# Delta rule of a four-layer kernel: sums for the norms of q and k on four column groups in two batches, and two steps of the query convolution one turn later

## The chip, the cores and the metric

The kernel runs on one core of a Trainium2 chip. The metric is the time of one execution on the device in microseconds, as the median of several runs. One core has TensorE (matrix products into PSUM), VectorE, ScalarE and GpSimd, and queues for transfers. The profile calls them PE (and PEld for its weight loads), DVE, ACT and POOL.

## The reference

Four layers run one after another on x with 8 samples of 512 tokens and 128 channels. The change touches one half of the last layer alone, a gated delta rule. Cut to what matters:

```python
q = _causal_dw_conv_silu(x @ Wq, conv_q).reshape(bsz, seq_len, H, KD)   # H = 8 heads, KD = 128
k = _causal_dw_conv_silu(x @ Wk, conv_k).reshape(bsz, seq_len, H, KD)
v = _causal_dw_conv_silu(x @ Wv, conv_v).reshape(bsz, seq_len, H, VD)   # VD = 32
q = _l2norm(q)        # x / max(sqrt(sum(x * x)), 1e-6), over the 128 numbers of a head
k = _l2norm(k)
def step(state, inp):
    q_t, k_t, v_t, a_t, b_t = inp
    retained = jnp.einsum('bhvk,bhk->bhv', state, k_t)
    state = a4 * (state - b4 * retained[..., None] * k_t[:, :, None, :]) + b4 * v_t[..., None] * k_t[:, :, None, :]
    o_t = jnp.einsum('bhvk,bhk->bhv', state, q_t)
```

All arithmetic is in float32. The convolution has four taps. The sums of squares of q and of k over a head's 128 numbers are what the change computes in another way.

## The kernel before

`delta_rule` splits the layer into 16 **units**: a sample of 512 tokens and four of its eight heads (`u // 2` is the sample, `u % 2` the half of the heads). A unit has 4 **chunks** of 128 tokens. The recurrence over 128 tokens becomes a triangular system per chunk. Its 32 x 32 blocks are inverted by small products (L2045, with VectorE's X and Y and ScalarE's F between them), and then the chunk is solved: L2088 multiplies by an inverted block, VectorE copies the result to `d_W` (L2371), L2081 takes it to the next block, VectorE subtracts it from `d_r` (L2368), four times over; then VectorE makes zz (L2374) and ze (L2377), and TensorE uses them in L2094 and L2098.

The order is written out as **turns**. `in_turn` walks through them, and every engine's program is that walk with only its own instructions. The list `INVERT` has NI = 9 steps, so 9 turns invert one chunk, and 36 turns a unit. While chunk n is inverted, chunk n - 1 is solved (`SOLVE`, also 9 steps), and chunk n + 1 is made (`make`, in turns 0, 3 and 6 of the nine): TensorE's L2030 and L2038, VectorE's `d_D` and `d_A` (L2316, L2321, L2326, L2329), ScalarE's `d_D` and its four copies of `d_A` (L2228), GpSimd's `d_D` (L2187) and its two products `d_M` (L2192), which the next chunk's inversion needs. I call nine such turns a **room**, and number the rooms of a unit 0 to 3, the turns in it 0 to 8. Room 0 solves the last chunk of the unit before, which has no ze and no L2098.

Around that, `pieces_at` puts the preparation of later units into turns, each with a place: 0 ahead of the solve step, 1 behind it, 2 at the end of the turn. For a unit there are eight **runs** (x = 0 to 7): q and k of each of four heads. For an even run (q) TensorE makes one product over 512 columns (L2132), ScalarE scales it into `d_conv` (L2259, step j = 0), VectorE adds the other three taps, one instruction each (L2409, steps j = 1 to 3, over 511, 510 and 509 columns), and ScalarE applies Silu. For an odd run (k) TensorE makes four products (L2136) and ScalarE applies Silu at once. GpSimd squares the result (L2214) into one of four buffers `d_sq`. Then TensorE adds the squares over the 128 partitions, one product each (L2144): its moving operand is the squares (512 columns), its stationary operand 8 columns of `picks` that pick the output row, so that eight products, accumulated in the bank `few`, leave eight rows. VectorE copies these rows out (L2442), and four products (L2148) turn them so that tokens lie on partitions.

Preparation runs some one and a half units ahead. For a unit inverted in rooms 0 to 3, each room holds one even and one odd run of a later unit: its sums stand in turn 3 (even x) and turn 5 (odd x), its convolution steps j = 0 to 3 in turns 4, 4, 5 and 7. The gates, the value products (L2121, L2122 in turn 4), the keys' transposes (L2162 in turn 7 of rooms 0, 2 and 3), the norm of the output and, for every second unit, the output projection (L2170 and L2175, in room 1) stand between.

Every engine works its list off strictly in order, and waits are semaphore counts. In GpSimd's list the squaring of run x waits until the sum that last read its buffer is done.

## Time and profile before

| what | us |
|---|---|
| median of 3 runs (lowest, highest) | 4025.28 (4021.14, 4027.91) |
| the profiled run | 4018.16 |
| its span on the core | 4016.4 |
| busy in the span: PE, DVE, ACT, POOL | 3464.0, 2409.0, 1597.0, 538.5 |
| stage of the delta units | from 2476 to about 3937 |

The profiled run has a time of its own, 1.8 us over its span, and stands 7.1 us under the median. A row of a timeline gives the start from the span's start, the duration, engine and line, output and inputs with their shapes, and how many records it merges; in brackets the idle time of the engine before it and what ended it. A product in float32 leaves two records, one for each of two passes (x8 is four products); a transpose leaves one.

### The profile page before, as it was taken

To read this page: it belongs to the slowest core of one execution; us is meant where nothing else is said; L and a number is where in the kernel's file an instruction comes from. 1 tells how busy PE (TensorE), PEld (TensorE's weight loads), DVE (VectorE), ACT (ScalarE), POOL (GpSimd) and SP (SyncE) were. 2 spreads that over 40 slices of the span, in tenths; PEclk is the share of its full clock that TensorE was granted. 3 is DMA by queue.
4 is the path that set the end of the run, shared out by engine and by line. 5 is a ranking of instruction groups with operands and counts; after the bars stand their busy time and mean duration, and the time that the engine had idled before them with its cause. 6 is when DMAs were issued, how large, how long until landed. Compare 5 with 4: busy or idle time off the path is not lost. (4 is left out here: it accounts for less than half of the span.)

```text
span 4016.4 us, 124072 instructions
## 1 busy us (share of the span) xinstructions
PE 3464.0 (86%) x55256; PEld 2180.0 (54%) x55256; DVE 2409.0 (60%) x6248; ACT 1597.0 (40%) x2941; POOL 538.5 (13%) x564
## 2 busy tenths in 40 slices
PE   3877777678999999999978796999999999999985
PEld 1336665224545555555556342666666666666772
DVE  3757777328777667767785112565666666666545
ACT  1663333345444444444320343444444344434323
POOL 0212222000000000000000000222222222222210
PEclk9986667789989888888765897999999999999967
DMA  2000000111111111111000001000000000000000
GB/s 89 0 0 1 1 1 1 44 65 59 45 34 45 42 45 37 41 44 35 14 3 3 16 0 44 2 3 3 2 3 2 3 2 3 3 3 3 2 2 23
DMA packets 37029, 77.11 MB, mean 19 GB/s; under 512 B 7696, under 2 KB 11152, under 8 KB 35472
## 3 DMA queue, kind: packets, MB, share of 16 engines
q1 hardware_dynamic: 36496, 69.17, 5.3%
q8 instruction: 437, 7.16, 0.7%
q14 instruction: 96, 0.79, 0.1%
HBM read 64.83 MB, written 4.33 MB: 17 GB/s over the span
## 5 line engine op out<-in xcount | busy, mean ns | idle before, releaser
L1369 PE MATMUL ps<-g_hs,g_fc 128*128 128x512 f32 x448 | 275.2, 699 | 55.1 <-DVE g_hs L1683 39.6
L1260 PEld LDWEIGHTS ps<-g_Q,g_K 32*32 32x32 f32 x12288 | 205.4, 120 | 184.1 <-issue 97.8
L1491 ACT ACTIVATE g_hidden<-ps 128x512 f32<-128x512 f32 x224 | 133.2, 595 | 419.4 <-PE ps L1369 417.7
L2136 PE MATMUL ps<-d_hp,d_w_k 128*128 128x512 f32 x512 | 280.3, 634 | 0.0
L1260 PE MATMUL ps<-g_Q,g_K 32*32 32x32 f32 (+1 forms) x12288 | 236.6, 227 | 27.4 <-DVE g_H L1529 10.1
L1383 PE MATMUL ps<-g_hidden,g_proj 128*128 128x512 f32 x448 | 256.6, 660 | 0.0
L2214 POOL TENSOR_TENSOR d_sq<-d_QK 128x512 f32<-128x512 f32 x128 | 133.7, 1044 | 912.8 <-ACT d_QK L2265 751.6
L2234 ACT ACTIVATE d_F<-ps 128x128 f32<-128x128 f32 x256 | 70.9, 277 | 347.4 <-PE ps L2045 344.2
L1228 POOL COPY g_xb<-X 128x512 f32<-128x512 f32 x8 | 7.3, 908 | 1217.4 <-DVE X L1689 1105.9
L2409 DVE SCALAR_TENSOR_TENSOR d_conv<-ps,w_conv_q,d_conv 128x511 f32<-128x511 f32 (+2 forms) x192 | 142.4, 742 | 36.8 <-ACT d_conv L2259 33.0
L2192 POOL TENSOR_TENSOR d_M<-d_A,w_joins 128x128 f32<-128x128 f32 (+1 forms) x128 | 114.3, 912 | 342.8 <-ACT d_A L2228 342.8
L2045 PE MATMUL ps<-d_X,d_M 32*32 32x32 f32 x8192 | 123.7, 196 | 39.7 <-DVE d_X L2341 20.0
L794 PE MATMUL ps<-att_kg,att_qx 32*128 32x96 f32 x1024 | 121.7, 354 | 42.0 <-DVE att_qx L708 27.4
L2038 PE MATMUL ps<-d_QK 128*128 128x128 f32 x1024 | 153.6, 295 | 0.0
L2368 DVE TENSOR_TENSOR d_r<-d_r,ps 32x128 f32<-32x128 f32 x192 | 55.0, 286 | 161.4 <-PE ps L2081 89.6
L2045 PEld LDWEIGHTS ps<-d_X,d_M 32*32 32x32 f32 x8192 | 96.2, 108 | 100.0 <-issue 66.0
L1276 PEld LDWEIGHTS ps<-g_V,g_KT 32*32 32x32 f32 x4096 | 81.1, 121 | 126.1 <-issue 91.6
L1517 DVE TENSOR_TENSOR g_S<-g_S,ps 128x128 f32<-128x128 f32 x64 | 18.4, 288 | 215.5 <-PE ps L1276 215.2
L1493 ACT ACTIVATE g_hidden<-g_hidden 128x512 f32<-128x512 f32 x224 | 141.1, 630 | 7.2
L794 PEld LDWEIGHTS ps<-att_kg,att_qx 32*128 32x128 f32 x1024 | 115.5, 254 | 51.0 <-DVE att_qx L708 29.7
L1369 PEld LDWEIGHTS ps<-g_hs,g_fc 128*128 128x128 f32 x448 | 78.3, 206 | 119.4 <-DVE g_hs L1683 42.8
L771 ACT ACTIVATE att_pt<-ps 96x512 f32<-96x512 f32 x128 | 75.0, 594 | 169.6 <-PE ps L811 168.7
(479 smaller groups left out, 7938.8 us busy)
## 6 DMA issues: line engine op xcount, KB each, us to landing
g_hs<-gate_rows SPq DMA_DIRECT2D x56, 256.0 KB, 3.4
g_fc<-in_c_fc_dram SPq DMA_DIRECT2D x56, 256.0 KB, 4.1
g_proj<-in_c_proj_dram SPq DMA_DIRECT2D x56, 256.0 KB, 2.6
X<-in_x_dram SPq DMA_DIRECT2D x1, 2048.0 KB, 10.8
w_c_fc<-in_c_fc_dram SPq DMA_DIRECT2D x1, 2048.0 KB, 7.9
w_c_proj<-in_c_proj_dram SPq DMA_DIRECT2D x1, 2048.0 KB, 12.3
ex_root<-gate_rows SPq DMA_DIRECT2D x1, 2048.0 KB, 15.7
h_rows<-k SPq DMA_DIRECT2D x1, 2048.0 KB, 6.2
```

Of the source, the lines that this page charges most:

```text
L794: ins = e.matmul(scored[:, g, b], qx[ts(g, 32), q, 4 * u + b, :, :].rearrange("p h q -> p (h q)"), kg[ts(g, 32), q, 4 * u + b, :], start=T ...
L1260: ins = e.matmul(later(scored, n_), keys_, queries(n_, planes, r_, 4 * i + j), start=(turn_ == 0 and part == 0 and n_ != 1), stop=(part == 1),
L1369: e.matmul(P[2], fc[:, n % 2, ts(f, C)], hs[:, n % 2], start=True, stop=True).then_inc(pe.steps, pe.did(now(f"u{i}")))
L1383: e.matmul(P[3], proj[:, n % 2, f, :], r[:, (16 * c["half"] + i) % 5], start=(c["half"] == 0 and i == 0), stop=(c["half"] == 1 and i == 15 ...
L1491: e.activation(r[:, slot], P[2], ACT.Relu).then_inc(act.steps, act.did(now(f"r{i}")))
L1493: e.activation(r[:, slot], r[:, slot], ACT.Square).then_inc(act.steps, act.did(now(f"q{i}")))
L2038: ins = e.matmul(mk[:, ts(h, C)], QK[:, 1, H, t], QK[:, part - 1, H, t], start=True, stop=True)
L2045: ins = e.matmul(inv[rows, h], stationary[rows, h], moving[rows, h], start=True, stop=True, tile_position=(32 * j, 32 * j))
L2136: ins = e.matmul(b, w_k[:, j, ts(H, C)], hp_of(u)[:, j:j + T], start=(j == 0), stop=(j == TAPS - 1))
L2192: e.tensor_tensor(M[:, a, levels], A32[:, a].unsqueeze(1).to_broadcast([C, many, 4, 32]), k.w["joins"][:, levels].unsqueeze(2).to_broadcas ...
L2214: e.tensor_tensor(squares(x), qk, qk, ALU.mult).then_inc(pool.steps, pool.did(f"{tag}sq{x}"))
L2409: e.scalar_tensor_tensor(cv[:, late:], tap_bank(run)[:, 0:T - late], k.w["conv_q"][:, 4 * g + run // 2, 3 - late:4 - late], cv[:, late:], ...
```

## The change

- **Sums.** `squares` is now put twice a unit instead of eight times: for x = 3 and x = 7, in the turn where the sum of that run stood (turn 5 of rooms 0 and 2). Each time TensorE issues four products, one for each buffer of `d_sq`, each with a stationary operand of 32 columns and on a column group of its own (`tile_position=(0, 32 * j)`), so that product j writes the 32 partitions from 32 j on. The first batch starts the accumulation, the second ends it. `picks` becomes two matrices of 32 columns, of which the first column or the second one is ones. The sum of run x comes to stand in row 32 * (x % 4) + x // 4.
- **Rows.** `d_square_rows` has 128 rows instead of 8, and VectorE copies all of `few`. The four products that turn them take a new table `heads` (128 x 8) as their moving operand instead of the 8 x 8 corner of the identity, and contract 128 rows.
- **Waits.** GpSimd's squares wait for the batch that read the four buffers.
- **Convolution.** VectorE's steps j = 1 and 2 are put one turn later: turns 5 and 6 instead of 4 and 5. Step 3 stays in turn 7.

```diff
-                        put(u, NI * (x // 2) - 50 + (0, 0, 1, 3)[j], "conv", TAPS * x + j, place=(1 if j == 0 else 2))
+                        put(u, NI * (x // 2) - 50 + (0, 1, 2, 3)[j], "conv", TAPS * x + j, place=(1 if j == 0 else 2))
...
-                    put(u, NI * (x // 2) - 42 + 2 * (x % 2), "squares", x)
+                    if x % 4 == 3:
+                        put(u, NI * (x // 2) - 42 + 2 * (x % 2), "squares", x // 4)
...
-                            e.wait_ge(pool.steps, pool.at(f"{tag}sq{x}"))
+                            e.wait_ge(pool.steps, pool.at(f"{tag}sq{4 * x + 3}"))
                             if x == 0 and u:
                                 e.wait_ge(dve.steps, dve.at(f"u{u - 1}ssq"))
-                            row = 4 * (x % 2) + x // 2
-                            e.matmul(few[0:8, :], k.w["picks"][:, row, :], squares(x), start=(x == 0), stop=(x == 7)).then_inc(pe.steps, pe.did(f"{tag}ss{x}"))
+                            for j in range(4):
+                                ins = e.matmul(few[ts(j, 32), :], k.w["picks"][:, x, :], squares(j), start=(x == 0), stop=(x == 1), tile_position=(0, 32 * j))
+                            ins.then_inc(pe.steps, pe.did(f"{tag}ss{x}"))
...
-                                ins = e.matmul(few[:, ts(i, 8)], sq_rows[:, ts(i, C)], k.w["ident"][0:8, 0:8], start=True, stop=True)
+                                ins = e.matmul(few[:, ts(i, 8)], sq_rows[:, ts(i, C)], k.w["heads"][:], start=True, stop=True)
...
-                                e.wait_ge(pe.steps, pe.at(f"{tag}ss{x - 4}"))
+                                e.wait_ge(pe.steps, pe.at(f"{tag}ss0"))
                             elif u:
-                                e.wait_ge(pe.steps, pe.at(f"u{u - 1}ss{x + 4}"))
+                                e.wait_ge(pe.steps, pe.at(f"u{u - 1}ss1"))
...
-                            e.wait_ge(pe.steps, pe.at(tag + "ss7"))
-                            e.tensor_copy(sq_rows[:], few[0:8, :]).then_inc(dve.steps, dve.did(tag + "rows"))
+                            e.wait_ge(pe.steps, pe.at(tag + "ss1"))
+                            e.tensor_copy(sq_rows[:], few).then_inc(dve.steps, dve.did(tag + "rows"))
```

Lines of the changed file are one to five higher than those of the kernel before. TensorE's list in room 0, turns 3 to 5, before the change; L2144 is a sum, L2132 the query's product, L2081 and L2088 belong to the solving, L2045 to the inversion, L2121 and L2122 are the value products:

```order
L2132 MATMUL ps<-d_hp,d_w_q 128x512
L2144 MATMUL ps<-d_sq,w_picks 8x512
L2081 MATMUL ps<-d_W,d_A 32x32 x4
L2045 MATMUL ps<-d_F,d_Y 32x32 x16
L2121 MATMUL ps<-d_w_v,d_hp 128x128 x4
L2122 MATMUL ps<-w_Wg,d_hp 128x128
L2088 MATMUL ps<-d_r,d_Y 32x32 x4
L2045 MATMUL ps<-d_X,d_M 32x32 x16
L2144 MATMUL ps<-d_sq,w_picks 8x512
L2081 MATMUL ps<-d_W,d_A 32x32 x4
L2038 MATMUL ps<-d_QK 128x128 x4
```

The same turns of TensorE after the change:

```order
L2133 MATMUL ps<-d_hp,d_w_q 128x512
L2082 MATMUL ps<-d_W,d_A 32x32 x4
L2046 MATMUL ps<-d_F,d_Y 32x32 x16
L2122 MATMUL ps<-d_w_v,d_hp 128x128 x4
L2123 MATMUL ps<-w_Wg,d_hp 128x128
L2089 MATMUL ps<-d_r,d_Y 32x32 x4
L2046 MATMUL ps<-d_X,d_M 32x32 x16
L2145 MATMUL ps<-d_sq,w_picks 32x512 x4
L2082 MATMUL ps<-d_W,d_A 32x32 x4
L2039 MATMUL ps<-d_QK 128x128 x4
```

The sum of turn 3 is gone, and that of turn 5 is a batch of four. In room 2 the same holds, with the sum of turn 3 ahead of the query's product instead of behind it. In rooms 1 and 3 both sums are gone.

VectorE's list in room 3, turns 4 to 7, before the change; L2409 is the convolution:

```order
L2409 SCALAR_TENSOR_TENSOR d_conv<-ps,w_conv_q,d_conv 128x511
L2371 COPY d_W<-ps 32x128
L2409 SCALAR_TENSOR_TENSOR d_conv<-ps,w_conv_q,d_conv 128x510
L2368 TENSOR_TENSOR d_r<-d_r,ps 32x128
L2326 TENSOR_TENSOR d_D<-d_D,d_gam 128x512
L2329 TENSOR_TENSOR d_A<-ps,d_D 128x512
L2341 TENSOR_TENSOR d_X<-d_X,ps 128x128
L2343 STREAM_TRANSPOSE d_Y<-d_X 128x128
L2416 TENSOR_TENSOR d_values_gates<-d_values_gates,d_kn 128x128
L2371 COPY d_W<-ps 32x128
L2374 TENSOR_TENSOR d_zz<-d_W,d_gam 128x128
L2377 TENSOR_TENSOR d_ze<-d_zz,d_end 128x128
```

The same turns of VectorE after the change:

```order
L2373 COPY d_W<-ps 32x128
L2411 SCALAR_TENSOR_TENSOR d_conv<-ps,w_conv_q,d_conv 128x511
L2370 TENSOR_TENSOR d_r<-d_r,ps 32x128
L2328 TENSOR_TENSOR d_D<-d_D,d_gam 128x512
L2331 TENSOR_TENSOR d_A<-ps,d_D 128x512
L2343 TENSOR_TENSOR d_X<-d_X,ps 128x128
L2345 STREAM_TRANSPOSE d_Y<-d_X 128x128
L2418 TENSOR_TENSOR d_values_gates<-d_values_gates,d_kn 128x128
L2411 SCALAR_TENSOR_TENSOR d_conv<-ps,w_conv_q,d_conv 128x510
L2373 COPY d_W<-ps 32x128
L2376 TENSOR_TENSOR d_zz<-d_W,d_gam 128x128
L2379 TENSOR_TENSOR d_ze<-d_zz,d_end 128x128
```

The first convolution step has moved from ahead of the `d_W` copy to behind it, and the second from ahead of `d_r` to between the scaling of the values and the next `d_W` copy. It is the same in the other rooms.

## Rows read from the trace of the kernel before

**Rows 1.** Windows: stretch, engines busy (records), PE clock, DMA share, GB/s
```profile
2529.00:3767.00 1238.00, 1187.97 (x22567) 843.04 (x22567) 765.04 (x2277) 509.00 (x1131) 324.65 (x314) 1.00 0.01 3
```

**Rows 2.** Timeline of a room 3, turns 5 to 8, all engines
```profile
3383.26 0.34 PE L2088 MATMUL ps<-d_r,d_Y 32*32 32x32 f32 x5
...
3384.37 0.29 DVE L2371 COPY d_W<-ps 32x128 f32<-32x128 f32 x1
...
3385.47 0.29 DVE L2368 TENSOR_TENSOR d_r<-d_r,ps 32x128 f32<-32x128 f32 x1
...
3386.59 0.69 DVE L2329 TENSOR_TENSOR d_A<-ps,d_D 128x512 f32<-128x512 f32 x1
...
3387.74 0.25 DVE L2416 TENSOR_TENSOR d_values_gates<-d_values_gates,d_kn 128x128 f32<-128x128 f32 x1
...
3388.68 0.29 DVE L2377 TENSOR_TENSOR d_ze<-d_zz,d_end 128x128 f32<-128x128 f32 x1
3388.69 1.82 POOL L2192 TENSOR_TENSOR d_M<-d_A,w_joins 128x128 f32<-128x128 f32 x2 [5.05 <-ACT d_A L2228]
...
3389.27 0.97 PE L2094 MATMUL ps<-d_zz,d_P 128*128 128x32 f32 x8
```

**Rows 3.** Timeline of a room 0, turns 3 and 4, TensorE
```profile
3317.41 0.60 PE L2144 MATMUL ps<-d_sq,w_picks 128*8 128x512 f32 x1
3317.41 0.44 PE L2081 MATMUL ps<-d_W,d_A 128*32 128x32 f32 x8
...
3318.36 0.45 PE L2045 MATMUL ps<-d_F,d_Y 32*32 32x32 f32 x32
```

**Rows 4.** Timeline of the attention stage: 16 products on four column groups
```profile
424.66 1.08 PE L819 MATMUL ps<-att_pt,att_vt 96*32 96x128 f32 x32 [0.68 <-ACT att_pt L771]
```

**Rows 5.** Timeline of a room 2, turns 3 to 6, all engines
```profile
3008.86 1.02 PE L2144 MATMUL ps<-d_sq,w_picks 128*8 128x512 f32 x2
...
3009.81 1.12 PE L2132 MATMUL ps<-d_hp,d_w_q 128*128 128x512 f32 x2
...
3010.87 0.44 PE L2081 MATMUL ps<-d_W,d_A 128*32 128x32 f32 x8
...
3011.24 0.45 PE L2045 MATMUL ps<-d_F,d_Y 32*32 32x32 f32 x32
...
3011.34 0.28 DVE L2368 TENSOR_TENSOR d_r<-d_r,ps 32x128 f32<-32x128 f32 x1 [2.07 <-PE ps L2081]
...
3012.93 0.34 PE L2088 MATMUL ps<-d_r,d_Y 32*32 32x32 f32 x5
...
3013.40 0.29 DVE L2371 COPY d_W<-ps 32x128 f32<-32x128 f32 x1 [0.37 <-PE ps L2088]
3013.55 0.60 PE L2144 MATMUL ps<-d_sq,w_picks 128*8 128x512 f32 x1
...
3014.70 0.29 DVE L2368 TENSOR_TENSOR d_r<-d_r,ps 32x128 f32<-32x128 f32 x1 [0.23 <-PE ps L2144]
```

**Rows 6.** Timelines of two rooms 1; the first row's room has output
```profile
3258.81 0.97 PE L2094 MATMUL ps<-d_zz,d_P 128*128 128x32 f32 x8
...
3339.45 0.75 DVE L2409 SCALAR_TENSOR_TENSOR d_conv<-ps,w_conv_q,d_conv 128x511 f32<-128x511 f32 x1 [0.62 <-ACT d_conv L2259]
...
3342.45 0.69 DVE L2329 TENSOR_TENSOR d_A<-ps,d_D 128x512 f32<-128x512 f32 x1
...
3344.89 1.08 PE L2094 MATMUL ps<-d_zz,d_P 128*128 128x32 f32 x8
```

**Rows 7.** Timelines where VectorE meets GpSimd: a room 0, the last unit
```profile
3326.70 1.05 POOL L2214 TENSOR_TENSOR d_sq<-d_QK 128x512 f32<-128x512 f32 x1
3326.96 0.93 DVE L2391 TENSOR_TENSOR d_O<-d_o,d_qn 128x128 f32<-128x128 f32 x1
...
3888.78 1.72 POOL L2192 TENSOR_TENSOR d_M<-d_A,w_joins 128x128 f32<-128x128 f32 x2 [10.49 <-ACT d_A L2228]
...
3888.79 0.59 DVE L2377 TENSOR_TENSOR d_ze<-d_zz,d_end 128x128 f32<-128x128 f32 x1
```

More of the change, by code:

```diff
@@ L123 @@
     "gla": ["W_in2", "b_in2", "W_qka", "b_qka", "W_v2", "b_v2", "W_y2", "b_y2", "W_out2", "b_out2", "h0", "gla_mask"],
-    "delta": ["conv_q", "Wv3", "Wg3", "Wab3", "Wo3", "A_log", "dt_bias", "conv_v", "o_norm_w", "joins", "eye32", "upto3", "ones3", "picks"],
+    "delta": ["conv_q", "Wv3", "Wg3", "Wab3", "Wo3", "A_log", "dt_bias", "conv_v", "o_norm_w", "joins", "eye32", "upto3", "ones3", "picks", "heads"],
     "mix": ["W_r3", "W_k3", "W_v3", "mu"],
@@ L1855, in delta_rule @@
         ssq = k.sb("d_ssq", [C, 2, NT, NH], stack=s)
-        sq_rows = k.sb("d_square_rows", [8, T], stack=s)
+        sq_rows = k.sb("d_square_rows", [C, T], stack=s)
         cv = k.sb("d_conv", [C, T], stack=s)[:]
@@ L2744, in layouts @@
     o["upto3"], o["ones3"] = o["upto"].copy(), o["ones"].copy()
-    o["picks"] = rows(np.eye(8, dtype=np.float32))
+    o["picks"] = rows(np.eye(2, 32, dtype=np.float32))
+    o["heads"] = np.zeros((C, 8), np.float32)
+    for x in range(8):
+        o["heads"][32 * (x % 4) + x // 4, 4 * (x % 2) + x // 2] = 1.0
     for n in "rkv":
```

## The prediction

> **What bounds the kernel now.** I read first the windows view of the delta stage's steady part, then the timelines of TensorE, VectorE and GpSimd in the four kinds of nine-turn room that follow one another there, and last the rows in which VectorE and GpSimd meet. TensorE is busy for 1188 of 1238 us at a granted clock of 1.00 (2.4 GHz) [rows 1], so TensorE looks like the bound. The timelines say that it is so only in stretches. In turns 2 to 4 of a room its bursts stand end to end. From turn 5 to turn 8 a second chain is as long: VectorE's `d_W` copy, the product L2081 that needs it, then r (L2368), `d_D` (L2326), `d_A` (L2329), X, transpose, scale, W, zz, ze, each right behind the other, and TensorE's L2094 behind ze [rows 2]. After L2094 TensorE again goes on without a gap to the next room, so what counts in a room is how much earlier or later L2094 starts. GpSimd's two `d_M` products (L2192) start beside ze, 2.10 us after `d_A` starts (3386.59 to 3388.69) [rows 2].
>
> **The sums, as work of TensorE.** One sum is two passes: 1.02 us for both [rows 5], 0.60 for one [rows 3], so 0.43 a pass and 0.855 a sum. Eight a unit and 16 units are 128 sums. Four sums on four column groups are not in the trace at 512 columns. The nearest row is L819: 16 products of 128 columns on four column groups, 32 records in 1.08 us [rows 4]. Serially they would be 32 passes of a quarter of 0.43, 3.4 us; with 0.27 of latency taken off, 0.81 remain, so all four groups ran at once. The other bound is no overlap, 3.42 us for a batch. I take 0.86, since L819 is the same kind of tiling with four different moving operands.
>
> **What the removed sums free, room by room.** The edit takes one sum out of turn 3 and one out of turn 5 of every room, and puts a batch into turn 5 of rooms 0 and 2.
> - Turn 3. In rooms 0, 1 and 3 the sum runs beside L2081, which uses another column group: both start at 3317.41, and L2045 follows at 3318.36 [rows 3]. L2081 alone takes 0.37, as from 3010.87 to 3011.24 [rows 5], so 0.95 becomes 0.37: 0.58 gained. In room 2 the sum stands ahead of the query's product and nothing is beside it: 3008.86 to 3009.81, 0.95 gained [rows 5].
> - Turn 5, room 3. Now VectorE does the first step of the convolution, then copies W (3384.37), and r follows at 3385.47. The copy could start 0.47 after L2088 (3383.26), as in room 2 (3012.93 to 3013.40) [rows 2, 5]. With L2088 0.58 earlier (3382.68) it starts at 3383.15; L2081 at 3383.49; the convolution's step now stands behind the copy, at 3383.47, and r comes 0.78 behind it, at 3384.25 instead of 3385.47. So `d_A` is 1.23 earlier. Here the moved step pays: it no longer stands ahead of the copy.
> - Turn 5, room 1. The convolution's first step waits 0.62 for ScalarE's copy until 3339.45, and the W copy waits behind it [rows 6]. Afterwards W and L2081 don't wait for that, but r stands behind the step, which starts at 3339.45 as before: r at 3340.23, and `d_A`, 1.12 after r (3385.47, 3386.59) [rows 2], at 3341.35 instead of 3342.45: 1.10 earlier.
> - Turn 5, rooms 0 and 2. The batch takes the sum's place and also holds the column group of L2081, which today runs beside the sum (from 3013.55 on) [rows 5]. L2081 now comes after it. r still gains, since it no longer waits for the sum's last pass: L2081 to r is 0.47 (3010.87, 3011.34) [rows 5]. In room 2 the batch starts at 3013.55 - 0.95 = 3012.60, L2081 at 3013.46, and that makes 3013.93 for r instead of 3014.70, 0.77 less; L2038 behind L2081 lets `d_A` gain 0.72 of it. In room 0, by the same steps from 0.58 instead of 0.95, it is 0.37.
>
> **What the moved steps cost.** The second step on VectorE goes from turn 5 to the end of turn 6, between scale and W. There VectorE has no gap: `d_A` 3386.59, scale 3387.74, then W, zz and, at 3388.68, ze [rows 2]. It takes 0.78 to its successor, but starts 0.11 closer behind scale than W does, so W, zz and ze come 0.67 later: W at A + 2.11, zz at A + 2.44, A being `d_A`'s start. Now the price of the meeting: zz and ze read two operands from SBUF, and GpSimd's first `d_M` product starts at A + 2.10. Where such a VectorE operation starts inside a GpSimd one, it waits for its end: L2391 takes 0.93 at 3326.96, while L2214 runs from 3326.70 to 3327.75; zz and ze, of the same shape, take 0.29 [rows 2]. And ze at 3888.79, just behind `d_M` at 3888.78, takes 0.59 [rows 7]. Today ze starts 0.01 ahead of `d_M`. The two `d_M` products take 1.72 together there; the second is four times as wide, and I estimate 0.46 and 1.26. With the change zz comes into the first one, gets through at its end, and ze meets the second. I put ze's end at A + 4.03 and L2094 at A + 4.08. In rooms 2 and 3 it stands at A + 2.68 now (3386.59, 3389.27) [rows 2], and in room 1 at A + 2.44 (3342.45, 3344.89) [rows 6]. So it is 1.40 later against A in rooms 2 and 3, and 1.64 in room 1. Room 0 has no ze: zz is ready at A + 2.75, 0.07 later, and L2391 no longer meets L2214, which gives 0.18 back. Where room 1 also holds the output projection (7 of its 15 rooms), L2175 waits for ScalarE and, with the product behind it, holds L2094 until 3258.81 [rows 6], which is later than ze in that room; I take ze as hidden there, and the 1.11 gained at `d_A` stay.
>
> This meeting is where the Trainium skill has a rule that speaks against the change. "SBUF — State Buffer", "Who interferes with whom": a VectorE instruction with two SBUF inputs and a GpSimd instruction that reads SBUF take one shared port pair as a lock, and the later one blocks fully. By that, the trace agrees: 0.93 and 0.59 instead of 0.29.
>
> **The sum.** Rooms with preparation beside them: 15 of kind 0, 15 of kind 1 (7 with output), 15 of kind 2, 14 of kind 3.
> - room 0: -0.37 + 0.07 - 0.18 = -0.48, x15 = -7.2
> - room 1: -1.10 + 1.64 = +0.54, x8 = +4.3; with output -1.11 x7 = -7.8
> - room 2: -0.72 + 1.40 = +0.68, x15 = +10.2
> - room 3: -1.23 + 1.40 = +0.17, x14 = +2.4
> - opening stretch before the first room: ten sums stand there, and three batches come for them. I take three sums of 0.95 [rows 5] as gained, -2.9. Bounds: 0, if ScalarE's chain sets the pace there, and 10 x 0.855 - 3 x 0.86 = 6 the other way.
>
> Together -1 us. The copy to `d_square_rows` takes 128 rows instead of 8, over the same 512 columns; the four products on `heads` contract 128 instead of 8 rows; one small load more goes out with the stage's weights. I take nothing for them, with a bound of 1 us a unit if the wider copy or product were slower. The profiled span is 4016.4, that run 4018.2, the median of three 4025.3. A difference of 1 us applied to the median gives **4024**.
>
> **The rivals.**
> - No meeting: zz and ze are not held, or `d_M` comes later than I think. Then L2094 stands at A + 3.11 at most: rooms give -0.48, -0.43 (-1.11), -0.29, -0.80, together -34, with the opening -37: 3988. For it: ze now passes just ahead of `d_M` and takes its 0.29 [rows 2]. Against: [rows 7].
> - zz loses (slower): it comes into the first `d_M` product only some 0.07 before the second claims its turn. If the second goes first, zz waits for both and ends at A + 3.85. This decides at zz later than about A + 2.5. Room 0 then pays 1.25 more, rooms 2 and 3 0.12, and room 1 without output 0.12 + 1.27, since GpSimd's L2201 slips in ahead of ze: +33 on the sum, 4057.
> - TensorE's work is the bound all along: 128 sums become 32 rounds, 96 x 0.855 = 82 us less, 3943. Against it: VectorE's unbroken chain in [rows 2].
> - The batch doesn't overlap, so that the change doesn't do what it says: 2.57 more in each of 30 rooms, 4101. Against it: L819 [rows 4].
>
> **How the numbers follow.** The forecast has a chance of 0.48, with 4010 to 4040 for itself (0.5 us a room of error in `d_A`, half of it cancelling); no meeting 0.22; zz loses 0.20; TensorE all along 0.05; no overlap 0.05. The range 3986 to 4058 leaves out the last two and the rims. Faster or slower by over 0.2% (8 us) is about what a measurement of this kernel can tell. Of the forecast's 0.48 I give 0.15 to faster, 0.21 to same and 0.12 to slower. Faster: 0.15 + 0.22 + 0.05 = 0.42; same 0.21; slower: 0.12 + 0.20 + 0.05 = 0.37.
>
> **What would show it.** In the changed profile: 8 records of a batch in about 1.1 us; turn 3 shorter by 0.58 in three rooms of four; W behind L2088 by 0.47; zz or ze with a mean well over 0.3 us, or `d_M` over 1.82 for the pair; L2094 at A + 4.1; in room 1 the W copy ahead of the step that waits for ScalarE. The prediction is wrong if zz and ze keep 0.29 us, if the batch takes over 2 us, if zz itself takes over 1 us, or if the granted clock falls below 1.00 in the steady part.

## The result: 3.8% slower, and where the time went

The changed kernel takes 4170.22 us (median of 4 runs, 4162.68 to 4201.56), the kernel before beside it 4023.21 us: a ratio of 1.038 (95% interval 1.033 to 1.044; it is taken over all runs, the two medians alone give 1.037). The forecast was 4024 us, in a range of 3986 to 4058. The profiled run of the changed kernel took 4168.27 us, with a span of 4166.5 us.

All of it lies in the delta stage while preparation still runs beside the inversion, that is in rooms 0 to 57. They take 1415.90 us from their first L2046 on, where they took 1259.84. (The spans differ by 150 us: 156 more in these rooms, 1 more in the opening of the stage, and 7 less ahead of it and behind the rooms.) This is the windows view of that stretch (its length, busy us and records of PE, PEld, DVE, ACT and POOL, then the granted clock of PE, the share of the DMA engines, GB/s), of the changed kernel:

```profile
2525.71:3941.61 1415.90, 1320.73 (x22889) 965.09 (x22890) 812.24 (x2314) 515.19 (x1153) 328.78 (x319) 0.88 0.01 2
```

The instructions are as many as before; TensorE is busy 112 us longer with them, and its granted clock is 0.88, where [rows 1] has 1.00. The clock has two levels, 1.2 and 2.4 GHz, and the mean hides a saw: in these rooms it fell 28 times to the lower level, for 3.4 to 17 us each, 352 us in all. The kernel before had one such fall there, of 6.8 us. Of the 28, none lies in a room 0, 13 in rooms 1, 7 in rooms 2 and 8 in rooms 3. At 23 of them TensorE waited for ze ahead of L2095 in the 4 us before. The other five are short (3.4 us) and lie in rooms 1 with the output projection, behind a wait for ScalarE ahead of L2177. The page of the changed kernel has it in its row of slices; the stage is the 26th to the 38th digit, and the kernel before has thirteen 9s there:

```profile
PEclk9886667888989899888657979798989898898867
```

**What VectorE and GpSimd do is as forecast.** A room 3 without a fall in it, timelines of VectorE, GpSimd and TensorE (start, duration, engine, line, operation; in brackets the idle time before and who ended it):

```profile
3386.93 0.29 DVE L2373 COPY d_W<-ps 32x128 f32<-32x128 f32 x1 [0.94 <-PE ps L2089]
3387.25 0.75 DVE L2411 SCALAR_TENSOR_TENSOR d_conv<-ps,w_conv_q,d_conv 128x511 f32<-128x511 f32 x1
...
3388.03 0.29 DVE L2370 TENSOR_TENSOR d_r<-d_r,ps 32x128 f32<-32x128 f32 x1
...
3389.15 0.69 DVE L2331 TENSOR_TENSOR d_A<-ps,d_D 128x512 f32<-128x512 f32 x1
...
3390.47 0.74 DVE L2411 SCALAR_TENSOR_TENSOR d_conv<-ps,w_conv_q,d_conv 128x510 f32<-128x510 f32 x1
...
3391.25 1.74 POOL L2194 TENSOR_TENSOR d_M<-d_A,w_joins 128x128 f32<-128x128 f32 x2 [3.82 <-ACT d_A L2230]
3391.57 0.29 DVE L2376 TENSOR_TENSOR d_zz<-d_W,d_gam 128x128 f32<-128x128 f32 x1
3391.90 1.23 DVE L2379 TENSOR_TENSOR d_ze<-d_zz,d_end 128x128 f32<-128x128 f32 x1
...
3393.19 1.08 PE L2095 MATMUL ps<-d_zz,d_P 128*128 128x32 f32 x8 [1.20 <-DVE d_ze L2379]
```

The `d_W` copy stands ahead of the convolution's first step; `d_M` starts at A + 2.10 (A is the start of `d_A`, 3389.15); zz gets through between its two products with its 0.29, and ze, which took 0.29 in [rows 2], meets the second and takes 1.23. L2095 (L2094 before) starts at A + 4.04; the forecast was A + 4.08. The groups by line and form over the same 58 rooms (count, busy us, mean ns, idle time of the engine ahead of it and its releaser) say that it is so in every room with a ze:

```profile
L2194 POOL TENSOR_TENSOR d_M<-d_A,w_joins 128x512 f32<-128x512 f32 x58 | 76.8, 1324 | 0.0
L2095 PE MATMUL ps<-d_zz,d_P 128*128 128x32 f32 x456 | 64.2, 286 | 46.3 <-DVE d_ze L2379 46.3
...
L2379 DVE TENSOR_TENSOR d_ze<-d_zz,d_end 128x128 f32<-128x128 f32 x43 | 53.1, 1235 | 1.5
```

TensorE now waits 46.3 us for ze ahead of L2095. In the kernel before the same group reads 0.0, since TensorE came to L2094 last:

```profile
L2094 PE MATMUL ps<-d_zz,d_P 128*128 128x32 f32 x456 | 56.3, 267 | 0.0
```

**The batches too.** TensorE in a room 2: eight records of a batch in 1.06 us, and L2082 starts 0.90 us after the batch does.

```profile
3363.76 1.06 PE L2145 MATMUL ps<-d_sq,w_picks 128*32 128x512 f32 x8
3364.66 0.41 PE L2082 MATMUL ps<-d_W,d_A 128*32 128x32 f32 x8
```

**What was not forecast stands right behind.** Windows over two rooms 3 of the changed kernel, one without a fall and one with, then the 4 us ahead of that fall and the stretch at the lower clock:

```profile
3378.22:3401.42 23.20, 21.19 (x408) 16.41 (x408) 14.11 (x44) 8.76 (x20) 5.33 (x6) 1.00 0.01 3
3470.04:3499.28 29.24, 27.23 (x408) 21.07 (x408) 15.01 (x46) 8.76 (x20) 6.34 (x6) 0.78 0.01 2
3482.21:3486.21 4.00, 2.80 (x37) 1.93 (x22) 3.39 (x6) 1.46 (x5) 1.73 (x2) 1.00 0.00 0
3486.21:3503.28 17.07, 17.07 (x162) 12.60 (x162) 5.71 (x23) 3.72 (x10) 2.30 (x2) 0.50 0.00 1
```

TensorE's timeline around that fall, at 3486.21:

```profile
3482.78 1.02 PE L2137 MATMUL ps<-d_hp,d_w_k 128*128 128x512 f32 x2
3485.01 1.08 PE L2095 MATMUL ps<-d_zz,d_P 128*128 128x32 f32 x8 [1.20 <-DVE d_ze L2379]
3485.92 1.64 PE L2099 MATMUL ps<-d_ze,d_KT 128*128 128x32 f32 x8
3487.49 0.65 PE L2046 MATMUL ps<-d_Y,d_F 32*32 32x32 f32 x32
3488.07 2.08 PE L2137 MATMUL ps<-d_hp,d_w_k 128*128 128x512 f32 x2
3489.94 3.46 PE L2077 MATMUL ps<-d_S,d_QK 128*128 128x32 f32 x16
```

Between two products of 512 columns, L2137 until 3483.8 and L2137 from 3488.07 on, TensorE waits 1.20 us and makes L2095, L2099 and a burst of L2046, all of them 32 columns wide. In the middle of that the clock falls, and L2137 then takes 2.08 instead of 1.02 us. Once at the lower clock, TensorE is busy all the time and is the bound, for 17 us; the room takes 29.24 us instead of 23.20, of which the late L2095 explains nothing, since both rooms have it. Nor does the order of the work, which is the same in both: why this room fell and the other one passed stays open.

Rooms 0 to 57 take 156 us more than before. By the rooms that have no fall, 11 us of it would be there at full clock too (the count is below). The rest, some 145 us, goes with 345 us more at the lower clock: 0.42 us lost for each.

One wait is the same in both kernels: in the seven rooms 1 with output TensorE waits 1.40 us for ScalarE ahead of the output projection, 9.8 us in all. Before, none of these rooms fell; in the changed kernel, which has no sums in them and other steps on VectorE, five of the seven did, and the same 28 records take longer (818 ns for 611). L2175 is of the kernel before, L2177 the same line of the changed one:

```profile
L2175 PE MATMUL ps<-d_OT,w_Wo 128*128 128x512 f32 x28 | 13.7, 611 | 9.8 <-ACT d_OT L2298 9.8
L2177 PE MATMUL ps<-d_OT,w_Wo 128*128 128x512 f32 x28 | 19.1, 818 | 9.8 <-ACT d_OT L2300 9.8
```

So a wait of that length doesn't by itself bring the clock down here.

### The profile page after: what moved, and what is told of

It is laid out like the page before. It is cut to its first block and busy times, and to the rows that moved or that the text cites. A ratio compares the mean times of both kernels' runs of the same rounds, so it can differ in the third digit from the quotient of the medians.

```text
span 4166.5 us, 124073 instructions
## 1 busy us (share of the span) xinstructions
PE 3571.1 (86%) x55256; PEld 2286.0 (55%) x55256; DVE 2442.8 (59%) x6248; ACT 1594.4 (38%) x2941; POOL 537.9 (13%) x564
## 5 line engine op out<-in xcount | busy, mean ns | idle before, releaser
L2137 PE MATMUL ps<-d_hp,d_w_k 128*128 128x512 f32 x512 | 338.4, 753 | 1.3 <-ACT d_QK L2267 1.3
L2046 PEld LDWEIGHTS ps<-d_X,d_M 32*32 32x32 f32 x8192 | 99.7, 111 | 116.4 <-issue 65.2
L2046 PE MATMUL ps<-d_X,d_M 32*32 32x32 f32 x8192 | 128.0, 199 | 40.0 <-DVE d_X L2343 24.3
L2226 ACT ACTIVATE d_D<-d_D 128x512 f32<-128x512 f32 x64 | 40.3, 629 | 315.6 <-DVE d_D L2318 315.6
L2077 PEld LDWEIGHTS ps<-d_S,d_QK 128*128 128x128 f32 x768 | 138.6, 271 | 35.0 <-issue 17.7
L2039 PE MATMUL ps<-d_QK 128*128 128x128 f32 x1024 | 155.9, 298 | 0.0
## 6 DMA issues: line engine op xcount, KB each, us to landing
w_c_proj<-in_c_proj_dram SPq DMA_DIRECT2D x1, 2048.0 KB, 12.4
```

Of the source, the lines that this page charges most:

```text
L2039: ins = e.matmul(mk[:, ts(h, C)], QK[:, 1, H, t], QK[:, part - 1, H, t], start=True, stop=True)
L2046: ins = e.matmul(inv[rows, h], stationary[rows, h], moving[rows, h], start=True, stop=True, tile_position=(32 * j, 32 * j))
L2077: ins = e.matmul(b[:, half * 128 + 32 * h:half * 128 + 32 * h + 32], QK[:, what, 4 * (u % 3) + h, ts(c, C)], S[:, 4 * g + h], start=True, ...
L2137: ins = e.matmul(b, w_k[:, j, ts(H, C)], hp_of(u)[:, j:j + T], start=(j == 0), stop=(j == TAPS - 1))
```

## The experiments

All ratios are against the kernel before, run beside them. "Falls" are those of the granted clock in rooms 0 to 57 of the profiled run, in rooms 0, 1, 2 and 3; the changed kernel has 0, 13, 7, 8.

| kernel | us | ratio, 95% interval | falls | us at lower clock |
|---|---|---|---|---|
| before | 4023.21 | | 0, 0, 0, 1 | 7 |
| changed | 4170.22 | 1.0382 (1.0326 to 1.0437) | 0, 13, 7, 8 | 352 |
| e1_sums_only | 4036.81 | 1.0048 (1.0025 to 1.0070) | 0, 11, 0, 0 | 130 |
| e2_steps_only | 4240.84 | 1.0553 (1.0519 to 1.0587) | 0, 11, 7, 10 | 369 |
| e3_masks_late | 4031.96 | 1.0009 (0.9994 to 1.0025) | 1, 13, 0, 0 | 140 |
| e4_twice | 4150.32 | 1.0310 (1.0283 to 1.0337) | 0, 12, 8, 5 | 304 |
| e5_pairs | 3999.48 | 0.9957 (0.9936 to 0.9978) | 0, 2, 0, 3 | 21 |
| e6_between | 4211.77 | 1.0450 (1.0383 to 1.0517) | 1, 15, 7, 3 | 348 |
| e7_split | 4080.40 | 1.0154 (1.0123 to 1.0184) | 0, 9, 7, 4 | 253 |
| e8_all | 4006.22 | 0.9979 (0.9961 to 0.9996) | 0, 3, 0, 6 | 41 |
| e9_hold | 4113.28 | 1.0235 (1.0212 to 1.0258) | 0, 4, 0, 1 | 17 |
| e10_steps_masks | 4105.98 | 1.0224 (1.0202 to 1.0246) | 0, 7, 5, 2 | 167 |
| e11_first_step | 4111.03 | 1.0217 (1.0187 to 1.0247) | 0, 15, 0, 11 | 311 |
| e12_pairs_first | 3995.99 | 0.9943 (0.9922 to 0.9964) | 1, 0, 0, 3 | 24 |

The falls are counted in one run of each kernel. The mean granted clock over the whole execution is on record for every run, and it bears the order out: 0.867 to 0.874 for the kernel before, 0.825 to 0.837 for the changed kernel, 0.825 to 0.833 for e2_steps_only, 0.850 to 0.859 for e1_sums_only, 0.864 to 0.872 for e5_pairs and 0.870 to 0.871 for e9_hold.

### One half of the change at a time

e1_sums_only, against the changed kernel:

```diff
-                        put(u, NI * (x // 2) - 50 + (0, 1, 2, 3)[j], "conv", TAPS * x + j, place=(1 if j == 0 else 2))
+                        put(u, NI * (x // 2) - 50 + (0, 0, 1, 3)[j], "conv", TAPS * x + j, place=(1 if j == 0 else 2))
```

> The changed kernel with the convolution's steps put back to turns 4, 4, 5 and 7: only the sums are changed against the kernel before. In the changed kernel the granted clock fell about 25 times in the steady part of the delta stage (none but one before), each time where TensorE waits for ze in turn 7 or 8. Theory A (the long wait alone): zz and ze no longer meet GpSimd's d_M, L2095 stands at A + 2.7 again, the wait is as short as before and the clock stays at 1.00; the rooms gain -0.37 (x15), -0.72 (x15) and -0.58 (x14), with -3 for the opening: about 3996 us. Theory B (the removed sums alone thin TensorE's work): the falls stay as many, with some 300 us at the lower clock and 4100 us or more. Theory C (both are needed): clock 1.00 and 3996, as theory A; the kernel with the moved steps alone tells A from C.

(Its first count was rough: of the 28 falls above, five don't stand at a wait for ze.)

e2_steps_only, against the kernel before:

```diff
-                        put(u, NI * (x // 2) - 50 + (0, 0, 1, 3)[j], "conv", TAPS * x + j, place=(1 if j == 0 else 2))
+                        put(u, NI * (x // 2) - 50 + (0, 1, 2, 3)[j], "conv", TAPS * x + j, place=(1 if j == 0 else 2))
```

> The kernel before with the convolution's steps in turns 4, 5, 6 and 7, and eight single sums as before. ze is held by the second d_M product, so that L2094 stands at A + 4.0 in rooms 1 to 3. By rooms at full clock: 0: -0.11 (x15), 1: +0.54 (x8), with output -1.11 (x7), 2: +1.40 (x15), 3: +0.76 (x14): +26, 4049 us. Theory A (the long wait alone lowers the clock): 25 falls as in the changed kernel, 4150 us or more. Theory B (the removed sums alone) and theory C (both needed): no more falls than in the kernel before, 4049 us.

The moved steps alone are worse than the whole change, 4241 us: theory A's number, 4150 or more, and theories B and C fall as they were put. But A isn't all of it, for the sums alone don't give 3996 us either. Rooms 2 and 3 have no fall without the moved steps (e1) and 17 with them (e2). Rooms 1 fell in both. In e1 four of their 11 falls lie in rooms with output, behind the 1.40 us ahead of L2177, and seven in rooms without output, behind a wait of 1.69 us. TensorE's timeline there:

```profile
3341.01 0.44 PE L2082 MATMUL ps<-d_W,d_A 128*32 128x32 f32 x8 [1.69 <-DVE d_W L2373]
3341.38 1.69 PE L2039 MATMUL ps<-d_QK 128*128 128x128 f32 x8
```

With no sum in turn 5 TensorE waits 1.69 us for the `d_W` copy, which stands behind the step that waits for ScalarE; before, TensorE waited 0.60 us for GpSimd's squares there, and then the sum filled the rest. The clock falls just then, at 3341.82, and L2039 takes 1.69 instead of the 1.16 us it has elsewhere. So there are two kinds of place: the wait ahead of L2095, made by the moved steps, and turns 5 to 8 of rooms 1, made thin by the removed sums.

### The meeting of ze and `d_M`

e3_masks_late, against the changed kernel (GpSimd, ahead of the two `d_M` products):

```diff
                             e.wait_ge(act.steps, act.at(f"a{n}"))
+                            m = NT * u + c - 2
+                            if m >= 0:
+                                e.wait_ge(dve.steps, dve.at("z" + chunk(m // NT, m % NT)))
```

> The changed kernel, and GpSimd starts the two d_M products only when zz and ze of the chunk being solved are done, so that they don't meet. ze takes 0.29 again and L2095 stands at A + 3.1. Theories A and C: the wait is short enough, no falls, rooms give -0.48, -0.43 (with output -1.11), -0.29 and about -0.3: 3988 to 3997 us. Theory B: falls stay, 4100 us or more. If d_M comes too late for the next room's first step (its first use is 3.5 us after L2095), the next room starts its inversion later and gives part of it back: up to 0.5 us a room, 30 us.

Groups by line and form of e3_masks_late, rooms 0 to 57:

```profile
L2095 PE MATMUL ps<-d_zz,d_P 128*128 128x32 f32 x456 | 63.6, 284 | 12.4 <-DVE d_ze L2382 12.4
...
L2382 DVE TENSOR_TENSOR d_ze<-d_zz,d_end 128x128 f32<-128x128 f32 x43 | 12.5, 291 | 1.5
```

ze is back at 0.29 us, the wait sinks from 46.3 to 12.4 us, and rooms 2 and 3 have no fall left. Nothing was taken away but the meeting, by starting a product later that nobody waits for yet: at full clock rooms 2 and 3 last 21.6 and 22.3 us in place of 22.6 and 23.2, and a room 1 without output 21.4 in place of 22.4. So of the 124 us that rooms 0 to 57 are shorter (1292.18 for 1415.90) the meeting's own length makes 0.94 x 36 = 34; the other 90 go with 212 us less at the lower clock, again 0.42 for each. What remains against the expected 3988 to 3997 us are 14 falls, 13 of them in rooms 1. They aren't at the wait of e1_sums_only, since the `d_W` copy stands ahead of the step here: seven lie in rooms without output, behind 1.11 us of waiting for X ahead of L2046 or 0.65 for ze ahead of L2095, and six in rooms with output, behind the 1.40 us ahead of L2177. (Its profiled run took 4061.89 us, 30 more than its median.)

e7_split, against the changed kernel: zz has a step of its own (`zz{n}`), and L2095 waits for that.

```diff
-                            e.wait_ge(dve.steps, dve.at(f"z{n}"))
+                            e.wait_ge(dve.steps, dve.at(f"zz{n}"))
                             for h in range(4):
                                 ins = e.matmul(b[:, 384 + 32 * h:416 + 32 * h], Pm[:, a, h], zz[:, g, h], start=True, stop=True)
                             if c < NT - 1:
+                                e.wait_ge(dve.steps, dve.at(f"z{n}"))
```

> The changed kernel, and L2095 waits for zz alone, L2099 for ze. zz is ready at A + 2.75, so that L2095 stands at A + 2.83, right behind L2137, and L2099 at A + 4.05; today they stand at A + 4.04 and A + 5.0. The rooms 1 (without output), 2 and 3 are 1.0 us shorter at full clock: about 21.3, 21.6 and 22.2. Theory D: the stretch from L2137 to the next L2137 shrinks from 3.75 to 2.8 us, near that of e3_masks_late (2.9), so some falls are left: 4010 to 4040 us. If d_M's meeting with ze were itself the cause of the falls and not the lateness of TensorE's work, they would stay: 4120 us.

It came out at 4080, between the two answers: L2095 moved up, 9, 7 and 4 falls were left in rooms 1, 2 and 3. Its rooms 2 and 3 without a fall last 22.2 and 22.8 us, not the 21.6 and 22.2 expected. The seven falls in rooms 2 tell most about the cause; they are alike, and one is at 3409.50. The 4 us ahead of it, windows, and TensorE's timeline:

```profile
3405.50:3409.50 4.00, 3.81 (x54) 2.85 (x53) 3.44 (x8) 1.47 (x4) 1.87 (x3) 1.00 0.00 0
```

```profile
3405.61 1.02 PE L2138 MATMUL ps<-d_hp,d_w_k 128*128 128x512 f32 x2
3406.57 1.08 PE L2095 MATMUL ps<-d_zz,d_P 128*128 128x32 f32 x8
3407.84 1.08 PE L2100 MATMUL ps<-d_ze,d_KT 128*128 128x32 f32 x8 [0.19 <-DVE d_ze L2380]
3408.85 0.45 PE L2046 MATMUL ps<-d_Y,d_F 32*32 32x32 f32 x32
3409.23 1.85 PE L2138 MATMUL ps<-d_hp,d_w_k 128*128 128x512 f32 x2
```

TensorE is busy for 3.81 of 4.00 us by its records, its only wait is 0.19 us, and the clock falls all the same. What is scarce in these 4 us is not records but wide products: one of 128x512 and the start of a second, and between them L2095, L2100 and L2046 with 32 columns. The Trainium skill, "TensorE: Matmul & The Clock Gate", section "HAM oscillation — how this bites in real kernels", asks of a kernel that TensorE have no long idle gap. This trace doesn't agree: no such gap exists at 3409.50, and the measurement decides.

### Is it the missing wide work, or the wait?

e4_twice, against the changed kernel:

```diff
+                            if j == 0 and run // 2 != 2:
+                                e.matmul(b, w_k[:, 0, ts(H, C)], hp_of(u)[:, 0:T], start=True, stop=True)
                             ins = e.matmul(b, w_k[:, j, ts(H, C)], hp_of(u)[:, j:j + T], start=(j == 0), stop=(j == TAPS - 1))
```

> The changed kernel, and in rooms 1 to 3 TensorE makes the first product of the key's taps twice (128x512, 0.86 us), right ahead of the wait for ze, where it stood idle for 1.20 us. The repeated product changes nothing in the result. If the lower clock is the whole surprise, and work in the wait keeps it up: rooms as the changed kernel's at full clock (18.4, 22.2 or 24.9, 22.6, 23.2), some +10 us against the kernel before, and 6 us for the seven rooms with output where that product isn't hidden: 4039 us with the clock near 1.00 in the steady part. If the falls have another cause than TensorE's thin work there, they stay: 4170 to 4200 us.

e6_between, against the changed kernel; `again` holds the operands of the first product, made ahead of L2095 as before:

```diff
                                 ins = e.matmul(b[:, 384 + 32 * h:416 + 32 * h], Pm[:, a, h], zz[:, g, h], start=True, stop=True)
+                            if c < NT - 1 and again:
+                                e.matmul(*again.pop(), start=True, stop=False)
```

> The changed kernel, and the first product of the key's taps is made twice in rooms 1 to 3, as in e4_twice, but the second time between L2095 and L2099 (43 times) instead of ahead of the wait for ze. e4_twice filled the wait and the clock fell all the same. Theory D (what counts is the time without wide products, and L2095 and L2099, 32 columns each, are thin although their records stand end to end): the product parts the thin stretch, the falls in rooms 2 and 3 go; 43 x 0.86 = 37 us are on the path; together 4033 + 37 = about 4070 us if room 1 loses its falls too, 4100 if its falls ahead of L2095 stay. Rival (the wait itself lowers the clock, whatever stands behind it): falls as in the changed kernel, 4190 us or more.

Both missed. e4_twice fills 0.86 of the 1.20 us of waiting and gains 20 us of the 147. e6_between gave 4212 against theory D's 4070 to 4100, which is the number of its rival (the wait itself, 4190 or more): the extra products cost their 37 us and 26 falls stayed. Taken alone these two speak against any theory of TensorE's work. Windows of the 4 us ahead of a fall of e4_twice, at 3461.83:

```profile
3457.83:3461.83 4.00, 3.65 (x52) 2.62 (x51) 2.65 (x5) 1.92 (x3) 2.13 (x2) 1.00 0.02 4
```

e9_hold puts in more, at both places: four products in place of the one, two ahead of the wait and two between L2095 and L2099. The last of them is the one that counts; `twice` is true in rooms 1 to 3 (43 times).

```diff
+                            if twice:
+                                again.append((b, w_k[:, 0, ts(H, C)], hp_of(u)[:, 0:T]))
+                                e.matmul(*again[0], start=True, stop=True)
-                            ins = e.matmul(b, w_k[:, j, ts(H, C)], hp_of(u)[:, j:j + T], start=(j == 0), stop=(j == TAPS - 1))
+                            ins = e.matmul(b, w_k[:, j, ts(H, C)], hp_of(u)[:, j:j + T], start=(j == 0), stop=(j == TAPS - 1 or twice))
...
+                            if c < NT - 1 and again:
+                                e.matmul(*again[0], start=True, stop=True)
+                                e.matmul(*again.pop(), start=True, stop=False)
```

> The changed kernel, and the first product of the key's taps is made four times in rooms 1 to 3 (43 times): twice ahead of the wait for ze, as in e4_twice, and twice between L2095 and L2099. With one extra product at either place the clock fell in rooms 2 and 3 as often as in the changed kernel (12 to 14 times against 12; e7_split fell there with TensorE busy for 3.2 of the last 3.4 us). Theory D (too little wide work around L2095, idle or not): with all three, rooms 2 and 3 keep the clock, 0 to 2 falls there; each lasts 22.6 + 1.7 = 24.3 and 23.2 + 1.7 = 24.9 us; room 1 keeps its falls ahead of L2095; together 4033 + 74 + some 50 for room 1, 4130 to 4160 us. Rival (the lower clock has nothing to do with wide work there): 12 falls stay in rooms 2 and 3, 4240 us or more.

(By the table above the counts for rooms 2 and 3 are 15 in the changed kernel, 13 in e4_twice and 10 in e6_between.)

Windows over its rooms 0 to 57, and over one room 3:

```profile
2531.00:3885.01 1354.01, 1283.10 (x23146) 905.19 (x23147) 814.40 (x2314) 515.91 (x1152) 328.66 (x319) 0.99 0.01 2
```

```profile
3438.97:3463.90 24.93, 23.77 (x414) 17.54 (x415) 14.12 (x44) 8.75 (x20) 5.33 (x6) 1.00 0.01 2
```

TensorE has 257 records more than in the changed kernel, in 62 us less: granted clock 0.99 for 0.88, and one fall in rooms 2 and 3 where there were 15. ze still takes 1.24 us and L2095 is as late as ever. So the meeting and the late L2095 cost only their length, some 34 us in all (see e3_masks_late), and the lower clock is what made them dear.

Against the changed kernel e9_hold has both less waiting and more wide work. The run that parts the two is e4_twice, which has the same wait. The group of the first product behind ze, rooms 0 to 57, e4_twice and then e9_hold:

```profile
L2095 PE MATMUL ps<-d_zz,d_P 128*128 128x32 f32 x456 | 60.7, 277 | 15.6 <-DVE d_ze L2381 15.6
L2097 PE MATMUL ps<-d_zz,d_P 128*128 128x32 f32 x456 | 60.7, 277 | 15.6 <-DVE d_ze L2388 15.6
```

15.6 us of waiting for ze in both, at the same place, with the same product made twice ahead of it. Only the two products behind it are new in e9_hold, and the falls go from 25 to 5, the time at the lower clock from 304 to 17 us. Here it is the work that keeps the clock, not a shorter wait.

e9_hold also bettered its own forecast of 4130 to 4160, since rooms 1 kept the clock too, but for 4 short falls. One product behind L2095 (e6_between, with the full wait of 1.20 us) left the 7 falls of rooms 2 and took those of rooms 3 from 8 to 3. So the amount seems to count; these runs don't tell how much.

### Which of the two steps

e11_first_step, against the changed kernel: (0, 1, 2, 3) becomes (0, 1, 1, 3).

> The changed kernel with the steps in turns 4, 5, 5 and 7: step 1 stands one turn later as in the changed kernel, step 2 again in turn 5, ahead of r. No step stands between scale and W, so zz and ze don't meet d_M and L2095 stands at A + 2.7. Against the changed kernel r is 0.78 later in rooms 1 and 3 and 0.39 in rooms 0 and 2. Rooms at full clock: 18.7, 22 or 25.7, 21.6, 22.6. If the meeting behind step 2 is the cause of the falls in rooms 2 and 3, these are gone and those of room 1 stay, as in e1_sums_only (4037 us): 4025 to 4050 us. If step 1 matters for the clock as well: above 4080 us.

4111 us, not 4025 to 4050. Rooms 2 lost their falls, as they should with ze back at 0.29 us and no wait ahead of L2095. Rooms 3 have 11 falls, nine of them at another place. TensorE in such a room 3, turns 5 to 7:

```profile
3463.83 0.43 PE L2089 MATMUL ps<-d_r,d_Y 32*32 32x32 f32 x8
...
3465.54 0.45 PE L2046 MATMUL ps<-d_X,d_M 32*32 32x32 f32 x32 [1.28 <-DVE d_X L2343]
```

With both steps ahead of r, X comes late and TensorE waits 1.28 us ahead of turn 7's L2046, with no sum in turns 3 and 5 of a room 3 any more; the clock fell at 3466.63. This is a third place of the same kind. The first step's move without the new sums was not run, so it is not shown whether both are needed for it.

e10_steps_masks: e2_steps_only with GpSimd's wait of e3_masks_late.

> The kernel before (eight single sums) with the convolution's steps in turns 4, 5, 6 and 7 as in e2_steps_only, which gave 4241 us, and GpSimd's d_M products behind ze, as in e3_masks_late. If the meeting of ze with d_M, by lengthening the wait ahead of L2094 from 0.04 to 1.20 us, was what made e2_steps_only slow: L2094 stands at A + 3.1, the wait is 0.3 us, rooms 18.7, 22.2 or 26.0, 22.1, 22.4, few falls: 4015 to 4035 us. If the later steps lower the clock in another way (they move work of VectorE alone), it stays above 4150 us.

4106 us. The meeting was worth some 130 us of what e2_steps_only lost (1.0224 for 1.0553), but 14 falls are left, 7 of them in rooms 2 and 3, where e3_masks_late has none with the same 12.4 us of waiting. Ahead of a fall at 3421.96 in a room 2:

```profile
3417.96:3421.96 4.00, 3.74 (x55) 2.83 (x54) 2.58 (x7) 2.40 (x5) 2.39 (x3) 1.00 0.02 4
```

That is a fall with eight single sums in place and 0.26 us of waiting. In e10_steps_masks the falls of rooms 1 and 2 come back 187.7 us apart, in every second unit; the units between have the output projection in room 1, so that they aren't alike. In the changed kernel alike rooms do differ: of the seven rooms 1 with output the falls hit five and spare two, and they come back at the same place after 587.1 us (2755.76, 3342.85, 3929.95). Something beside the work in the room and its waits decides, and these runs don't show what. Why it hits e10_steps_masks and spares e3_masks_late stays open too.

### A version that keeps the wide work spread

e5_pairs, against e1_sums_only: four rounds of two sums, one in turn 5 of every room, in place of two rounds of four.

```diff
-                    if x % 4 == 3:
-                        put(u, NI * (x // 2) - 42 + 2 * (x % 2), "squares", x // 4)
+                    if x % 2 == 1:
+                        put(u, NI * (x // 2) - 42 + 2 * (x % 2), "squares", x // 2)
...
-                            for j in range(4):
-                                ins = e.matmul(few[ts(j, 32), :], k.w["picks"][:, x, :], squares(j), start=(x == 0), stop=(x == 1), tile_position=(0, 32 * j))
+                            for j in range(2):
+                                ins = e.matmul(few[ts(j, 32), :], k.w["picks"][:, x, :], squares(2 * x + j), start=(x == 0), stop=(x == 3), tile_position=(0, 32 * j))
```

> Convolution's steps as in the kernel before (turns 4, 4, 5, 7), and the sums in four rounds of two (q and k of one head, on column groups 0 and 1) in turn 5 of every room, so that rooms 1 and 3 keep a product of 512 columns there and only turn 3 loses its sum. In e1_sums_only nearly all falls of the clock (10 of 11 up to 3800) stood in room 1, 10.1 to 14.9 us into it, where TensorE had lost both sums and waited 1.4 to 1.7 us. Theory D (a stretch without wide products lowers the clock, and room 1 had two wide products fewer there): no falls in room 1, rooms give -0.35, 0, -0.7, -0.1: about 4005 us. Rival (the missing sum of turn 3 is enough, or the falls have another cause): falls in room 1 stay, 4025 us or more.

```profile
2525.84:3768.47 1242.63, 1176.84 (x22888) 861.46 (x22889) 779.80 (x2314) 515.89 (x1152) 328.66 (x319) 0.99 0.01 3
```

3999 us, faster than the kernel before by 0.4% (0.2 to 0.6). Rooms 1 fell twice instead of 11 times. TensorE's waits there are as long as in e1_sums_only: in a room 1 without output 1.19 us ahead of the pair and 0.55 ahead of turn 7's L2046, against 1.69 in one piece; none of the eight such rooms fell, where seven had. The rooms at full clock are no longer than those of e1_sums_only: 18.2, 21.9, 20.7 to 20.9 and 22.4 us, against 18.7, 21.9, 21.6 to 21.9 and 22.5 before. It makes twice as many rounds as the changed kernel. TensorE in its room 3, turn 5:

```profile
3283.31 1.05 PE L2145 MATMUL ps<-d_sq,w_picks 128*32 128x512 f32 x4 [0.34 <-POOL d_sq L2216]
3283.81 0.44 PE L2082 MATMUL ps<-d_W,d_A 128*32 128x32 f32 x8
```

A pair leaves two column groups free, and L2082 starts 0.50 us after it, beside its second pass; behind a batch of four it started 0.90 us after. The pair itself waits for GpSimd's squares, 0.34 us here, 18.2 us in all.

e12_pairs_first is e5_pairs with step 1 one turn later in rooms 1 and 3: `((0, 0, 1, 3) if x % 4 == 0 else (0, 1, 1, 3))[j]`.

> e5_pairs (3999 us), with step 1 of the convolution one turn later in rooms 1 and 3 alone, where it stood ahead of the W copy. If VectorE's chain still sets turn 5 there, r is 0.3 to 0.4 us earlier in both: 30 rooms, -10 us, 3989 us. If TensorE is the bound in turn 5 there with the pair's 0.86 us ahead of L2046 (its step lasts 2.94 us in room 3 of e5_pairs and of e8_all alike, with different places of step 1), nothing comes of it: 3996 to 4003 us.

3996 us, 0.9943 (0.9922 to 0.9964) of the kernel before, and 0.9957 for e5_pairs: no difference beyond the intervals. The rival's number came, but its reason isn't what the timelines show. In rooms 3 VectorE has the `d_W` copy and the steps 1 and 2 ahead of r in either order, end to end, and the rooms last 22.51 for 22.44 us. In rooms 1 r waits for TensorE's pair and L2082, and the pair waits 1.19 us for GpSimd's squares; the rooms last 21.83 for 21.89. So turn 5 is set there by VectorE's three operations and by GpSimd's squares, not by TensorE.

e8_all: pairs, all steps late, L2095 on zz alone, and `d_M` behind ze.

> Pairs as in e5_pairs, steps in turns 4, 5, 6 and 7 as in the changed kernel, L2095 on zz alone as in e7_split, and the d_M products behind ze as in e3_masks_late. L2095 at A + 2.83, L2099 at once behind it, A earlier in rooms 1 and 3 by some 0.6 (the pair in turn 5 holds no column group of L2082). Rooms at full clock: 18.4, 21.2 (24.9 with output), 21.2, 22.0. Theory D: stretch of 2.6 us as in the kernel before, no falls in the steady part: 3985 to 3995 us. Rival (something else than the thin stretch): falls in room 1 as in e3_masks_late, 4020 us.

4006 us, 0.998 of the kernel before and outside its 3985 to 3995. At full clock rooms 1 last 22.2 us (25.9 with output) and rooms 3 22.7, instead of the 21.2 (24.9) and 22.0 expected: r waits for L2082 and the pair, and the pair for GpSimd's squares, 17.9 us in all. 9 falls are left, of 3.4 to 10.2 us. So the moved steps no longer cost 5% once nothing meets and the wide work is spread, but they bring nothing either: every kind of room without output is longer than in e5_pairs, by 0.04 us in rooms 0 and about 0.3 in the others.

## Why the prediction was wrong, by its own steps

The rooms of the changed kernel that passed without a fall can be held against the sum term by term.

| term | forecast | at full clock |
|---|---|---|
| room 0 | -0.48 | 18.38 for 18.74: -0.36 |
| room 1, no output | +0.54 | 22.4 for 21.9: +0.5 (see below) |
| room 1, output | -1.11 | 24.89 for 25.99: -1.10 |
| room 2 | +0.68 | 22.56 for 21.85: +0.71 |
| room 3 | +0.17 | 23.20 for 22.51: +0.69 |
| opening | -2.9 | not at full clock in either kernel; as it ran, 54.59 for 53.35: +1.2 |
| the whole | -1 | about +11, and +1 in the opening |

No room 1 without output passed at full clock in the changed kernel; the value is e9_hold's 24.11 less its two products of 0.86 on the path, and e4_twice has two such rooms of 22.39. The opening is taken from the stage's first product (L2132 or L2133, 2475.93 and 2471.12) to the first L2046 (2529.28 and 2525.71).

- **Right: the batch.** 0.90 for 0.86 us. The rival of no overlap is out.
- **Right: turn 3 and turn 5.** The turn with the sum taken out lasts 1.81 for 2.39 us, the 0.58 of [rows 3]; the `d_W` copy stands 0.47 behind L2089 in room 3 (3386.46, 3386.93); in room 1 it stands ahead of the step that waits for ScalarE.
- **Right: the meeting.** zz 0.29, ze 1.24, L2095 at A + 4.04. The first `d_M` product takes 0.46 and the second 1.32; 0.46 and 1.26 were estimated. Both rivals on it are out: zz neither escapes nor loses.
- **Wrong size: room 3.** The room of [rows 2] was one of three that last 22.94 us; ten others last 22.5 to 22.6. In it `d_A` was 0.43 us late already, so that 0.4 of the 1.23 gained was no gain elsewhere. Times 14 rooms that is 6 of the 9 us between the +2 that the forecast gives for the rooms and the +11 measured. One look at the length of all rooms of a kind ahead of reading one of them would have shown it.
- **Not borne out: the opening.** Two batches stand there, not three: the third comes in turn 5 of the first room 0. TensorE was busy for 45.4 us of it instead of 48.9, and it lasted 1.2 us longer all the same, with 15 us at the lower clock instead of 5. What sets its pace was not looked into.
- **The step that failed: "what counts in a room is how much earlier or later L2094 starts".** It prices a wait of TensorE by its length, and takes the 1.00 of [rows 1] as given for the changed kernel. The sum is worked out for a kernel at 2.4 GHz throughout. The added waits and the removed wide products brought the clock down 28 times, and this cost some 145 us; with the clock held by extra products, as in e9_hold, the same meeting and the same late L2095 went without it. The prediction had "if the granted clock falls below 1.00" in its last sentence as a condition, without a rival, a price or a chance.

Could the trace of before have shown it? Windows of before, in the steady part, behind it where the last unit has no preparation beside it, and the one fall in the steady part:

```profile
3700.00:3750.00 50.00, 48.26 (x936) 34.98 (x934) 29.91 (x94) 18.86 (x44) 11.66 (x11) 1.00 0.01 3
3800.00:3850.00 50.00, 44.15 (x848) 39.91 (x848) 22.65 (x78) 16.45 (x37) 7.84 (x8) 0.69 0.01 2
2767.61:2774.44 6.83, 6.83 (x62) 3.81 (x60) 1.23 (x5) 2.77 (x8) 0.00 (x0) 0.50 0.01 4
```

The same inversion and solving, without the products of 512 columns between them, ran at 0.69 while TensorE was busy for 44 of 50 us. And one of 58 rooms fell with all sums in place. (TensorE also waits more in the second row, 5.85 us for 1.74, so it doesn't part work from waits.) Both rows suggest that the 1.00 was held with the help of the preparation's wide products, with little to spare, and the change makes 32 rounds of 128 single products. A rival "the clock falls in the rooms that lose both sums or wait longer" belonged among the cases, with that row for its price.

The likeliest case's mechanism, the meeting, was right and its total was not; of the rivals, none was this one.
